# GpSimd clears a dead buffer between its row sends, in place of waits for TensorE's points

## The reference

```python
proj = x @ W_in.T                       # xp, z, B, C, dt
scores = einsum(C, B) * Lm * dt         # within a chunk of 64
y = scores @ xp + C @ state(before the chunk) * decay + xp * D_param
y = rmsnorm(y) * norm_w * silu(z)
x = layernorm(x + y @ W_out.T)
logits = -|x - keys|^2 + x @ rw.T + rb
topv, topi = top_k(logits, 4);  w = softmax(topv)
x = layernorm(x + sum_k w_k * (gelu(x @ w1[topi_k].T + b1) @ w2[topi_k].T + b2))
```

## Time and profile before

| | us |
|---|---|
| median of 3 runs | 379.04 |
| lowest, highest | 378.26, 385.06 |
| the profiled execution's own time | 381.55 |
| its span, first to last instruction | 379.7 |
| TensorE matmul busy | 298.3 (79%) |
| VectorE, ScalarE, GpSimd busy | 185.6, 214.1, 153.6 |

### The profile page before, as it was taken

The page is one execution under the profiler, slowest core; times in us unless marked ns, Lnnn a source line. Parts: engine busy times, 40 slices in busy tenths (PEclk is TensorE's granted clock), DMA queues, the critical chain, the costliest instruction groups (busy, mean ns, idle before and its releaser), DMA issues.

```text
span 379.7 us, 11577 instructions
## 1 busy us (share of the span) xinstructions
PE 298.3 (79%) x3492; PEld 267.3 (70%) x3493; DVE 185.6 (49%) x817; ACT 214.1 (56%) x763; POOL 153.6 (40%) x167
## 2 busy tenths in 40 slices
PE   4987997594949575273679557999999989999883
PEld 4975776282737464163679557999999989998662
DVE  3154576071534436225357444566555645674163
ACT  2635588062443515313268334688888868898345
POOL 4025002607162433462655645566555545543300
PEclk9958999687786859565989958899999999999998
DMA  7999100101010110120212211222222222220194
GB/s 241 236 378 415 70 3 9 55 3 54 9 40 24 33 33 18 45 70 30 71 45 75 61 51 52 61 77 71 69 68 72 68 58 73 62 47 12 59 381 118
DMA packets 25407, 32.44 MB, mean 85 GB/s; under 512 B 4315, under 2 KB 18292, under 8 KB 25104
## 3 DMA queue, kind: packets, MB, share of 16 engines
q1 hardware_dynamic: 20576, 22.38, 20.1%
q0 software_dynamic: 4352, 8.79, 6.8%
q10 hardware_dynamic: 432, 0.67, 0.7%
HBM read 20.84 MB, written 11.50 MB: 85 GB/s over the span
## 4 chain that ended last, share of the span: by engine, by line
PE 66%; issue 11%; another core or an unknown queue 7%; ACT 7%; DVE 3%; DMA 3%; ACTq 0%; SPq 0%; DVEq 0%; POOLq 0%; POOL 0%
PE bank L762 15%; PE bank L783 14%; PE bank L576 5%; PE bank L561 5%; PE bank L757 4%; ACT hs L1575 3%; PE bank L747 2%; PE bank L622 2%; PE bank L773 2%; PE bank L548 2%; DMA w1s<-yrows 2%; PE bank L847 1%; PE bank L532 1%; ACT shared L1738 1%
## 5 line engine op out<-in xcount | busy, mean ns | idle before, releaser
L1899 POOL DMA_INDIRECT yrows<-shared,idi x72 | 78.4, 1089 | 70.1 <-issue 40.5
L1831 POOL DMA_INDIRECT xrows<-rows_all,sli x64 | 61.9, 968 | 106.6 <-issue 44.5
L1738 ACT ACTIVATE shared<-bank,shared 128x128 f32<-128x128 f32 x256 | 73.0, 370 | 30.2 <-PE bank L762 19.9
L783 PE MATMUL bank<-w2s,shared 128*128 x512 | 70.8, 283 | 9.8 <-ACT shared L1738 9.8
L762 PE MATMUL bank<-shared 128*128 128x128 f32 x512 | 73.1, 289 | 0.4 <-issue 0.4
L783 PEld LDWEIGHTS bank<-w2s,shared 128*128 128x128 f32 x512 | 65.2, 199 | 10.5 <-issue 10.4
L762 PEld LDWEIGHTS bank<-shared 128*128 128x128 f32 x512 | 67.2, 205 | 0.9 <-issue 0.6
L1388 DVE COPY shared<-w1s 128x644 f32 x64 | 32.1, 502 | 28.0 <-issue 27.2
L576 PE MATMUL bank<-shared 32*64 32x128 f32 x512 | 23.5, 344 | 13.5 <-DVE hx L954 6.9
L1724 ACT ACTIVATE shared<-bank 128x128 f32<-128x128 f32 x72 | 21.0, 292 | 22.5 <-remote 17.4
L747 PE MATMUL bank<-cst,shared 128*128 128x128 f32 x72 | 20.9, 291 | 13.2 <-ACT shared L1724 8.6
(11 more groups left out here) (239 smaller groups left out, 518.1 us busy)
## 6 DMA issues: line engine op xcount, KB each, us to landing
shared<-xrows SPq DMA_DIRECT2D x64, 70.0 KB
w1s<-in_w1T SPq DMA_DIRECT2D x1, 4128.0 KB, 23.0
w2s<-in_w2T SPq DMA_DIRECT2D x1, 4096.0 KB, 22.9
w1s<-yrows SPq DMA_DIRECT2D x8, 512.0 KB, 7.4
yrows<-shared,idi POOLq DMA_INDIRECT x72
xrows<-zrow SPq DMA_DIRECT2D x1, 1120.0 KB, 11.8
w1s<-in_b SPq DMA_DIRECT2D x1, 1024.0 KB, 22.5
xrows<-rows_all,sli POOLq DMA_INDIRECT x64
```

Source lines behind the costliest of these rows:

```text
L783: m = mm(out_bank(u), hT[u][:, f * P:(f + 1) * P], w2s[:, bass.ds(ex, 1), f, :], start=(f == 0), stop=(f == FB - 1))
L1738: m = act(hT[u][:, f * P:(f + 1) * P], hidden_bank(u)[:, f * P:(f + 1) * P], ACT.Gelu, bias=w[:, F + f:F + f + 1])
L1831: po.indirect_dma_start(out=xrows, out_offset=bass.IndirectOffsetOnAxis(ap=sli[:, g, k:k + 1], axis=0), in_=rows_all[:, g, :], in_offset=N ...
L1899: po.indirect_dma_start(out=yrows, out_offset=bass.IndirectOffsetOnAxis(ap=idi[r][:, 0:1], axis=0), in_=yw[r][:, :], in_offset=None, bound ...
```

## The change

For pairs 0 to 3 (`NP - 4` is 4) the waits of `paced` are gone. In their place, ahead of every send but the first, GpSimd sets the 512 columns of `gs` to zero, after it has waited for the clearing before this one. Pair 4 keeps its paced sends.

```diff
             def send(m_):
                 ready(m_)
                 for i in range(2 * TOPK):
-                    if m_ < NP - 3:
+                    if 0 < i and m_ < NP - 4:
+                        po.wait_ge(gm_set, 9 + 7 * m_ + i - 1)
+                        po.memset(gs[:], 0.0).then_inc(gm_set, 1)
+                    if m_ == NP - 4:
                         paced(m_, i)
                     send_one(m_, i)
```

## The result

| | before | after |
|---|---|---|
| median of the runs in pairs, us | 382.05 | 358.3 |
| lowest, highest | 378.26, 448.55 | 356.89, 362.52 |
| the profiled execution, its span | 381.55, 379.7 | 362.52, 360.7 |

The ratio is 0.945, with a 95% interval of 0.936 to 0.954: faster, about 21 us of 379. The ratio compares the faster, undisturbed runs alone and so leaves out 385.06 and 448.55 of before and 362.52 of after, which is the profiled execution and the slowest of its four. A later set of runs on another chip turned the sign round; it stands last among the experiments, and what comes before it holds for the chips on which the kernel before takes 378 to 385 us.

What follows compares the result with a forecast made beforehand. TensorE bounds the kernel, its signals held while dense sends pile up. Four windows of 10.40 + 8 x 0.45 = 14.0 us start pair 4 56.0 us after pair 0 instead of 84.2, gaining 28.2: 351 us, range 344 to 361.

Steps and rivals of the forecast that it cites:

- A send occupies something for 1.46 us, and sends closer than that pile up: GpSimd's sends, 1.26 us apart, pile up and hold TensorE and its signals; 1.46 us for each send.
- Waits removed, price 0.: Pairs 0 to 3: 28 waits go, six in seven already met, the seventh delaying only the eighth send; price 0.
- Clearing: a send every 1.83 us.: GpSimd's trains of pairs 0 to 3: 0.96 + 0.52 + 0.30 + 0.05 us between sends, 1.73 to 2.28.
- Toll per spaced send 0.45 us, at worst 0.75: TensorE's loss in the first stage for each send with none piled before it: 0.45 us, bounds 0 and 0.75.
- The seam.: From pair to pair: TensorE's window priced eight sends at 0.45 us, while GpSimd's train counted 7 x 1.83 us.
- VectorE beside the clearings, 0.: VectorE beside GpSimd's 28 memsets in pairs 0 to 3: cost taken as 0, at most 6 us.
- Everything behind keeps its length.: From pair 4's paced sends through pairs 5, 6, 7 and the experts to the end: order, lengths and holds unchanged.
- B: Each send costs TensorE 1.46 us however far from the next: window 22.1 us, time 383 us; chance 0.10.
- C: Signals stay held to the end of the longer train: 14.3 us in place of 10.2, time 395 us; chance 0.06.
- E: TensorE's holds have another cause and only coincide with sends: time unchanged, 379 us; chance 0.05.
- D: A few matmuls pass in each gap, about 1.0 us lost a send: window 18.4, time 369 us; chance 0.10.
- not faster: Whole kernel: within 7.6 us of no change (B and E), chance 0.15, or slower (C), chance 0.06.

Runs made afterwards that it cites:

- chip B: Second of three chips used, where the kernel before takes 378.83 us; it ran the copy, two clearings, and the spacing of more pairs.
- pairs 0 to 5: Against the change, clearings also space the sends of pairs 4 and 5 and the seams, and pair 4 has no waits: 347.84 us, ratio 0.915.
- chip C: Third chip used, where the kernel before takes 309.98 and 312.51 us; the change itself took 320.15 us there, ratio 1.031.
- the longest form: Kernel of pairs 0 to 5 with copies in place of clearings, sends 1.78 us apart, run on chip C: 336.46 us, ratio 1.085.
- all pairs: Against pairs 0 to 5, clearings also between the sends of pair 6, and between pair 7's rows and the experts' results: 349.0 us, ratio 0.911.

## Why the prediction was right, and where not

Where a hold exists, the mechanism was right. The forecast was 351 us with 344 to 361 as its own range, the time is 358.3. For the profiled execution it was 353.3, and 362.52 was measured. Of these 9.2 us, 4.4 lie between the first sends of pairs 0 and 4 (60.4 in place of 56.0), 3.7 in the later first send, and 1.1 behind pair 4's.

*A send occupies something for 1.46 us, and sends closer than that pile up*. Three runs bear it out: no relief at 1.26 us (22.1 us a window), none at 1.46 (21.1), relief at 1.67 (15.15). This was the step on which the forecast rested. What it is that a send occupies, no run shows.

*Waits removed, price 0.* Off by a little: alone they cost 1.5%. The prediction saw that the eighth send would come sooner, and asked only who waits for that send; it didn't count that this send joins the train and lengthens the hold by 1.46 us. With the clearings in there is no such train, so the price should be gone; no run keeps both. The prediction also read the eighth send's delay as 0.6 to 1.9 us; its start moved by 0.6 to 1.6, since the usual gap of 0.30 is part of the 1.86.

*Clearing: a send every 1.83 us.* Mis-sized: 1.67. The 0.54 us were as taken from the clearings of the start, but the gap of 0.30 ahead of a send shrinks to 0.17 behind a GpSimd operation; the row that showed it (0.20) was read as "about whole". It is below the prediction's lower end of 1.73 and still above the edge.

*Toll per spaced send 0.45 us, at worst 0.75*. Measured (15.15 - 10.40) / 8 = 0.59. This is the term that was too small: windows of 15.15 us in place of 14.0 are 4.6 us over four pairs. Nor is it one number: counted over the sends that lie in the four windows, the same spacing on chip B gave 0.48 (pairs 0 to 5), and two clearings, 2.25 us apart, 0.35. In the 0.59 is half clock: the two long windows have clocks of 0.81 and 0.80 and TensorE busy for 14.56 and 14.40 us of work that takes 10.76 in the first. The stops are many and short, and a standstill of 1.42 us, at the seam, stands ahead of the matmuls at half clock in the first of them; but with the seams closed one window still had a clock of 0.89. The prediction forecast over 0.9 in these windows; two in four had it.

*The seam.* The sum priced all eight sends of a pair as spaced, though the diff, and the prediction's own train of 7 x 1.83 us, space seven. A slip, small in time: closing the seam gave 14.9 in place of 15.15.

*VectorE beside the clearings, 0.* Right: 8.58 to 9.01 us busy a window, before 8.55 to 8.93.

*Everything behind keeps its length.* Right: 232.9 against 231.8 us, with pair 4's hold of 6.83 us included.

*The rivals.* B (the price belongs to the send) is refuted: the windows would be 22 us. C (nothing passes before the train is over) too: VectorE had its signal at 69.49, within the first train. E (another cause) by the runs with the waits removed and with the clearings ahead. D (half relief, 1.0 us a send) lay on the side of the miss, but 0.59 is nearer to the forecast's 0.45. The Trainium skill (SBUF — State Buffer, Who interferes with whom) says that PE and ACT never wait on anyone for their SBUF ports. On chip C nothing speaks against it; on the others TensorE waits, and the runs don't show on what.

*What the prediction couldn't see:* its rows come from one chip, and that the result came from one with holds was a condition that it didn't name. Its case "not faster" had an engine or a wait in it and never the chip on which the thing to be cured isn't there. There GpSimd's train sets the end, which the prediction did name as the second bound: it put the four trains at 53.6 us, and 52.3 was measured on chip C.

## What to carry to other kernels

When an engine stutters beside DMAs that another engine issues by software, compare a window with and without them, and trains of several lengths: the cost of one falls out of the difference, and says how far apart they have to stand. Here a spacing at that time gained nothing, one 0.21 us above it nearly all, and a filler that only writes left VectorE alone. All of the spacing is paid by the issuing engine, so stop where it becomes the bound. Measure such a cure on more than one chip before it is kept: here it is worth 5 to 9% where the holds exist, and costs 3% (8.5% in the longest form) where they don't.

## What was not expected

- Chips of one kind differ by 70 us in the same program (379 to 385 against 310 to 313), 42 of them in the stretch of the first four pairs, where sends 1.26 us apart hold TensorE on some and not on the other.
- The edge is hard: at a spacing of 1.46 us the ratio is 0.9985, at 1.67 it is 0.94.
- On chip C a shorter clearing costs as much as the full one.
- The gap ahead of a send is 0.30 us behind another send and 0.17 behind a clearing or a copy.
- On chips with holds the kernel for pairs 0 to 5 has the lowest median of the study, 347.84 us, though all pairs (349.0) can't be told from it; on the chip without, it is the kernel before, unaltered. No version that beats both kernels on both kinds of chip was found.
